# First cross attention of a two-layer block: two heads on 64 rows each, scores between two maxima, and one pair of maxima in eight copied by ScalarE

## The reference

```python
q = x @ Wq + bq            # x: 1024 rows of 128
k = y @ Wk + bk            # y: the context rows
v = y @ Wv + bv
scale = 1.0 / jnp.sqrt(D_HEAD)                 # D_HEAD = 16, 8 heads
weight = jnp.einsum('bhqd,bhkd->bhqk', q, k) * scale
weight = jax.nn.softmax(weight, axis=-1)
out = jnp.einsum('bhqk,bhkd->bhqd', weight, v)
return out.transpose(0, 2, 1, 3).reshape(B, SQ, D_EMBED) @ Wo + bo
```

## Time and profile before

| | us |
|---|---|
| median of 3 runs | 2700.87 |
| lowest and highest | 2694.35, 2701.8 |
| the profiled execution | 2705.45 |
| its span in the trace | 2703.7 |

### The profile page before, as it was taken

How to read it: one execution, slowest core, us unless ns; L and a number is a source line. 1 busy time by engine, 2 the same in 40 slices (tenths; PEclk the granted TensorE clock), 3 DMA queues, 4 the chain that set the end, 5 groups by cost and what they waited for, 6 DMA issues and landing times. The chain is left out here.

```text
span 2703.7 us, 33636 instructions
## 1 busy us (share of the span) xinstructions
PE 2405.5 (89%) x10214; PEld 876.6 (32%) x10272; DVE 2045.3 (76%) x3008; ACT 1513.5 (56%) x1842; POOL 301.9 (11%) x333
## 2 busy tenths in 40 slices
PE   6888677999999979999586599999999999997998
PEld 3555411222222224444222133323333333332443
DVE  5676688999995224344697888989999998976775
ACT  5555486777677843333332576666666666653111
POOL 5665500000000000000164000000000000000000
PEclk8898957999999989999698599999999999998998
DMA  5354371221000159954124331122013111111100
GB/s 144 127 167 143 130 113 31 67 63 31 26 24 27 31 104 211 217 153 121 32 73 98 78 91 30 30 63 72 29 30 105 30 30 30 30 36 69 47 1 8
DMA packets 200960, 198.63 MB, mean 73 GB/s; under 512 B 18525, under 2 KB 159362, under 8 KB 200086
## 3 DMA queue, kind: packets, MB, share of 16 engines
q1 hardware_dynamic: 200674, 196.69, 28.1%
q10 hardware_dynamic: 144, 0.10, 0.0%
HBM read 152.01 MB, written 41.48 MB: 72 GB/s over the span
## 5 line engine op out<-in xcount | busy, mean ns | idle before, releaser
L2768 DVE TENSOR_TENSOR y_acc<-y_acc,y_probs 128x1024 f32<-128x1024 f32 x400 | 486.7, 1217 | 35.2 <-ACT y_probs L2456 23.1
L2456 ACT ACTIVATE y_probs<-y_E,y_mask_bias 128x1024 f32<-128x1024 f32 x408 | 433.7, 1113 | 71.9 <-PE y_E L2548 63.9
L1223 ACT ACTIVATE x_probs<-x_E 128x1024 f32<-128x1024 f32 x408 | 397.1, 1024 | 135.8 <-PE x_E L1283 133.6
L1406 DVE TENSOR_REDUCE x_maxima<-x_M 128x1 f32<-128x496 f32 x660 | 410.2, 668 | 27.8 <-PE x_M L1265 17.2
L2557 PE MATMUL y_O<-y_probs,y_values 128*64 128x512 f32 x1632 | 400.2, 611 | 0.0
L2547 PE MATMUL y_E<-y_qa,y_ks 128*128 128x512 f16 x816 | 313.4, 384 | 1.5 <-ACT y_copied L2429 1.2
L2548 PE MATMUL y_E<-y_qb,y_ks 66*128 66x512 f16 x816 | 311.6, 382 | 0.0
L2429 ACT ACTIVATE y_copied<-y_M 128x1024 bf16<-128x1024 f32 (+1 forms) x164 | 162.5, 991 | 212.7 <-PE y_M L2511 212.7
L2706 DVE TENSOR_REDUCE y_maxima<-y_M 128x2 f32<-128x1024 f32 (+2 forms) x195 | 231.2, 1185 | 41.3 <-PE y_M L2511 32.3
L1874 DVE TENSOR_TENSOR f_hidden<-f_act_out,f_spread 128x512 f32<-128x512 f32 x160 | 110.7, 692 | 176.0 <-ACT f_act_out L1705 106.1
L1296 PE MATMUL x_O<-x_probs,x_values 128*32 128x512 f32 x1632 | 218.1, 607 | 0.7 <-ACT x_probs L1223 0.4
(11 more groups left out here) (499 smaller groups left out, 3154.6 us busy)
## 6 DMA issues: line engine op xcount, KB each, us to landing
f_spread<-comb_dram SPq DMA_DIRECT2D x160, 256.0 KB, 7.0
y_values<-v_dram SPq DMA_DIRECT2D x208, 128.0 KB, 2.2
v_dram<-a_v_out SPq DMA_DIRECT2D x26, 512.0 KB, 2.6
k_dram<-a_k_parts SPq DMA_DIRECT2D x26, 512.0 KB, 3.4
x_values<-v_dram SPq DMA_DIRECT2D x100, 128.0 KB, 2.2
f_weights<-f_w_in SPq DMA_DIRECT2D x40, 256.0 KB, 10.1
y_ks<-k_dram SPq DMA_DIRECT2D x75, 128.0 KB, 2.9
ssm_c_rows<-c_dram SPq DMA_DIRECT2D x16, 512.0 KB, 3.6
```

Source lines behind the costliest of these rows:

```text
L1223: nc.scalar.activation(probs[:, n % 2, 2 * g:2 * g + 2, :], psE[:, 2 * g:2 * g + 2, :], ACT.Exp).then_inc(exped, 1)
L1406: V.tensor_reduce(maxima[:, 2 * h + j, qt, c:c + 1], psM[(2 * entry + j) % 3][:, 0:CHUNK0], AX.X, ALU.max).then_inc(max_done, 1)
L2456: A(probs[:, i, :], psE[:, 2 * (i % 2):2 * (i % 2) + 2, :].rearrange("p a b -> p (a b)"), ACT.Exp, bias=mask_bias[:, bass.ds(c * TILES_IN_ ...
L2768: ins = V.tensor_tensor(acc[:, u % 2, :], acc[:, u % 2, :], probs[:, i, :], ALU.add)
```

## The change

There are four parts.

1. Keys and queries stand two heads together. A head has two groups of 64 rows, `low` 0 and 1, and the first head of a pair lies on partitions 0 to 63, the second on 64 to 127 (`row_place`). A score is then the sum of two matmuls on 64 rows (`low` 0 starts the bank, `low` 1 adds), and two heads run side by side: 8 matmuls on 64 rows in a tile take the place of 4 on 128. The maxima read `low` 0, and `qm` is gone. Loads of keys and queries are cut in two by head.
2. The order on TensorE in a tile is now: use, scores of the next tile (both g), use, values, and a third use if there is one.
3. A "max" use that is second in its tile, and whose pair is number 2 or 3 of 8, becomes "spare": ScalarE copies its two banks to bf16 (`copy_spare`, between its two exponentials of the next tile; two instructions where the banks don't adjoin), and VectorE merges the copy with one elementwise maximum into `spare_max`, in place of two reductions. There are 33 spares in the four units.
4. `give_maxima` gains a reduction of `spare_max` (units 1 to 3) and one or two memsets. GpSimd clears `spare_max`, three times.

```diff
                 def scores(u, t, g):
                     n = TILES0 * u + t
                     if n:
                         e.wait_ge(exped, 2 * n + g - 1)
-                    for j in (2 * g, 2 * g + 1):
-                        ins = T.matmul(psE[:, j, :], key_tile(4 * (u // 2) + j, t), qs[:, u, j, :],
-                                       start=True, stop=True)
-                    ins.then_inc(scored, 1)
+                    for low in range(2):
+                        for j in range(2):
+                            r = slice(64 * j, 64 * j + 64)
+                            ins = T.matmul(psE[:, 2 * g + j, :], key_tile(2 * (u // 2) + g, low, t)[r, :], qs[r, u, low, g, :],
+                                           start=(low == 0), stop=(low == 1))
+                            if low:
+                                ins.then_inc(scored, 1)
...
                 def free_banks(entry):
-                    e.wait_ge(max_done, max(2 * entry - 1, 0))
+                    for before in (entry - 2, entry - 1):
+                        if before in spare_number:
+                            e.wait_ge(spare_copied, spare_number[before] + 1)
+                    e.wait_ge(max_done, max(taken_before[entry] - ((entry - 1) not in spare_number), 0))
...
-                            scores(nu, nt, 0)
-                            if len(uses) == 3:
+                            if uses:
                                 use_banks(u, *uses.pop(0))
-                            scores(nu, nt, 1)
-                        if len(uses) == 2:
+                            for g in range(2):
+                                scores(nu, nt, g)
+                        if uses:
                             use_banks(u, *uses.pop(0))
                         weigh(u, t)
-                        if uses:
-                            use_banks(u, *uses.pop(0))
+                        for use in uses:
+                            use_banks(u, *use)
...
+                def copy_spare(entry):
+                    n = spare_number[entry]
+                    e.wait_ge(spare_mm, 2 * n + 2)
+                    if n >= 2:
+                        e.wait_ge(spare_merged, n - 1)
+                    out = spare[:, n % 2, :, :]
+                    banks = spare_banks(entry)
+                    heads = 2 // len(banks)
+                    for b, scores in enumerate(banks):
+                        ins = nc.scalar.activation(out[:, b:b + heads, :], scores[:, :, 0:CHUNK0], ACT.Copy)
+                    ins.then_inc(spare_copied, 1)
...
                         weights(u, t, 0)
+                        for kind, entry, _, _ in before[SPARE_AT:SPARE_AT + 1]:
+                            if kind == "spare":
+                                copy_spare(entry)
...
+                def merge_spare(n):
+                    e.wait_ge(spare_copied, n + 1)
+                    e.wait_ge(spare_cleared, spare_pair[n] // PAIRS)
...
+                    V.tensor_tensor(mine, mine, spare[:, n % 2, :, :], ALU.max).then_inc(spare_merged, 1)
...
+                def take_spares(u, entry):
+                    merge_spares_until(entry)
+                    e.wait_ge(spare_merged, spares_through(u))
+                    V.tensor_reduce(maxima[:, 0:4:2, 2:4, CHUNKS0].rearrange("p j q -> p q j"), spare_max[:], AX.X, ALU.max)\
+                        .then_inc(spare_taken, 1)
...
                         for kind, entry, pair_unit, pair in in_tile.get((u, t), ()):
+                            merge_spares_until(entry - 1)
```

More of the change, by code:

```diff
@@ L100, with row_place, load_queries, load_key_rows @@
 QS_ROWS = ((0, 0), (16, 1), (32, 0), (48, 0), (64, 2), (96, 1))
-QM_PARTS = (0, 1, 0)
-def load_far_queries(engine, k, d, u, loaded):
+LOW_ROWS = 64
+def row_place(r, head):
+    return r // LOW_ROWS, LOW_ROWS * head + r % LOW_ROWS
+def load_queries(engine, k, d, u, head, loaded):
     hg, cols = u // 2, slice(HALF * (u % 2), HALF * (u % 2) + HALF)
     rows = d.q0_dram[64 * hg:64 * hg + 64, :, cols]
[L108 to L119, removed]
-            .then_inc(loaded, 16)
[L123 to L138, removed]
+    for row, part in QS_ROWS:
+        low, r = row_place(row, head)
+        src = rows[:, part, :].rearrange("(h two f) n -> two f h n", f=16, two=2)[head]
+        engine.dma_start(k.qs[r:r + 16, u, low, :, :], src).then_inc(loaded, 16)
+def load_key_rows(sp, d, out, pairs, cols, row, part, loaded):
+    src = d.k0_dram[:, part, cols].rearrange("(h two f) n -> two f h n", f=16, two=2)
+    for head in range(2):
+        low, r = row_place(row, head)
+        sp.dma_start(out[r:r + 16, :, low, :], src[head][:, pairs, :]).then_inc(loaded, 16)
+def load_key_ones(sp, d, out, cols, loaded):
+    for head in range(2):
+        low, r = row_place(M_ROW0, head)
+        sp.dma_start(out[r:r + 16, :, low, :], d.key_ones[:, cols].unsqueeze(1).to_broadcast([16, 2, cols.stop - cols.start]))\
+            .then_inc(loaded, 16)
+KEY_PIECES = len(K_ROWS) + 1
 class Filler:
@@ L282, in _ @@
                 sp.dma_start(real[0:CTX, REST], d.real_keys[REST].partition_broadcast(CTX)).then_inc(spread_rest, 16)
[L283 to L286, removed]
+                for row in (80, 112):
+                    for head in range(2):
+                        low, r = row_place(row, head)
+                        sp.dma_start(k.qs[r:r + 16, :, low, :, :], d.x0_zeros).then_inc(zeroed, 16)
                 def store_k1(n):
@@ L1115, in _, with load_keys @@
             def _(sp):
-                def load_keys(heads, cols, loaded):
-                    for r, part in K_ROWS:
-                        load_key_rows(sp, d, ks[:, heads, cols], heads, cols, r, part, loaded)
-                    load_key_ones(sp, d, ks[:, heads, cols], cols, loaded)
-                near, far = slice(0, 4), slice(4, 8)
+                def load_keys(pairs, cols, loaded):
+                    for row, part in K_ROWS:
+                        load_key_rows(sp, d, ks[:, pairs, :, cols], pairs, cols, row, part, loaded)
+                    load_key_ones(sp, d, ks[:, pairs, :, cols], cols, loaded)
+                near, far = slice(0, 2), slice(2, 4)
                 sp.wait_ge(k.q_rest, 32)
```

137 lines of the change are left out of this document (88 added, 49 removed).

## The result

The changed kernel takes **2725.66 us** (median of 4 runs, 2723.55 to 2729.05), against 2699.43 us for the kernel before in as many runs: a ratio of 1.0096, interval 1.0076 to 1.0117. It is 26.2 us slower, where the forecast was 16.0. The profiled execution took 2726.0 us, its span 2724.0.

A forecast was written before the change was run, and what follows sets the result against it. TensorE was taken to set the tile, VectorE 0.24 us behind. Terms -19.0 - 0.6 + 29.0 + 6.6 = +16.0 us took the median from 2700.87 to 2716.9 us, 8-in-10 range 2690 to 2738.

The forecast's parts named there:

- the end of the maxima: End of each unit's maxima: TensorE waits for the 2.2 us reduction and memsets; +6.6 us in sum, bounds 2 to 8.
- the plain tile: Two-maxima tile in units 0 to 2: 2.43 us instead of 2.60, -19.0 us over 112 tiles.
- unit 3: Unit 3 keeps its loop between scores and exponentials, alternating 2.20 and 1.97 us; no change, stays at 109 us.
- 64 rows and order, units 0 to 2: Two shape-change gaps vanish on TensorE: -19.0 us in 112 plain tiles, -0.6 us in twelve three-maxima tiles.
- The spare: ScalarE's copy between exponentials and VectorE's merge delay TensorE: 0.59 + 0.27, say 0.88 us each, +29.0 us for 33.
- The three waits: Behind a spare: next maxima at 2.83 instead of 2.43 us, second scores 3.73 instead of 3.47, merge 0.27 more.
- A: At spares: next maxima and second scores don't wait for the copy; sum -13.0 us, 2688 us; chance 0.17.
- B: At spares: only the wait for the copy costs, 33 x 0.40 = 13.2 us; sum +0.2, 2701 us; chance 0.25.
- C: On TensorE: gaps stay between equal 64-row shapes, so rows and order gain nothing; 2736 us; chance 0.10.
- D: On TensorE: weight loads on 64 rows show, making a tile 0.45 us longer; 2785 us; chance 0.03.
- The signs: Expected in the trace: VectorE's share in units 0 and 1 from 94% to about 88%, each lasting about 150 us.
- The loads: Twice as many key pieces of half size, hidden by 12 us ahead of first use: cost nothing; uncovered, 1 or 2 us.

The follow-up runs named there:

- the ends alone: Changed kernel with no pair copied or merged, but the 1,984-element reduction and GpSimd's clears kept: 2705.82 us, ratio 0.9994 to the kernel before.
- the shorter end: Changed kernel with the merge one entry earlier, GpSimd's memset behind the split, and the spare_max reduction in three steps: 2716.17 us, ratio 1.0053 to before.

## Why the forecast was right in kind and 10 us short

The sign, the mechanism and the range held (2725.7 in 2690 to 2738). Of the four terms of the sum the end of the maxima was badly off and the plain tile slightly; unit 3, forecast unchanged, was off too. This is the sum with what the stretches and tiles gave, the gain from before to the kernel without spares, the losses from that to the changed one:

| term | forecast | measured |
|---|---|---|
| 64 rows and order, units 0 to 2 | -19.6 | -15.3 |
| the same, unit 3 | 0 | +1.1 |
| spares | +29.0 | +26.0 |
| end of the maxima | +6.6 | +12.5 |
| first tile, and rounding | 0 | +0.7 |
| sum | +16.0 | +25.0 |

**The plain tile, 2.43 forecast, 2.46 found.** Its reasoning held: maxima to scores is 0.22 (662.83 to 663.05), so equal shapes have no gap, and the second maxima wait for the hand-over of the bank, 1.15 us behind the first (1.14 forecast). The last term was misread. Values to the next maxima is 629.00 to 630.00 in the earlier trace rows, 1.00 us, and is 1.00 here (664.29 to 665.29); I took 0.98 "less rounding", which no row gives. With the 0.01 of the hand-over that is 0.03 us, over 112 tiles 3.4 us, most of the term's miss. Another 0.6 is the tiles with three maxima, which kept their 3.62 us where 3.57 was forecast. The measured -15.3 and +26.0 are themselves uncertain by about 1 us each, as the profiled execution without spares was spared the low clock at the start of unit 0. Of two readings of the same row, the shorter was the one I hoped for.

**Unit 3, forecast unchanged, 1.1 us longer.** Its longer step is 2.23 us in the mean of 21 tiles (890.91 to 893.15, below, is one of 2.24) instead of 2.21, which is half of the 1.1; the rest is some 0.1 us in each of the few tiles that are longer anyway. The shorter step stays 1.97. Unit 3 is the same without spares, so the difference comes with the 64-row scores. Why the loop between scores and exponentials is 0.02 us longer stays open.

```profile
885.92 1.07 PE L1343 MATMUL x_O<-x_probs,x_values 128*32 128x512 f32 x8
...
887.89 1.07 PE L1343 MATMUL x_O<-x_probs,x_values 128*32 128x512 f32 x8
...
890.91 1.06 PE L1343 MATMUL x_O<-x_probs,x_values 128*32 128x512 f32 x8
...
893.15 1.06 PE L1343 MATMUL x_O<-x_probs,x_values 128*32 128x512 f32 x8
```

**The spare, 0.88 forecast.** Measured 0.84 with a one-instruction copy (3.05 and 2.71 against twice 2.46) and 0.90 with two. The three waits are where they were placed: next maxima 2.91 us behind the first (2.83), the tile after the next at 5.81 (5.72), and the merge at 0.26 in its own experiment (0.27). The total is smaller than 33 times that, because four spares are not paid for so: two in the last tile of a unit cost nothing, as no maxima wait behind them, and two lie in the tile behind an end and are counted there. The other 29 took 26.0 us, 0.90 each. So the term came out 3.0 us too high, which hid a part of what the ends cost more; that is luck. Where the tile behind has 3.13 us, the merge costs 0.39, not 0.25.

**The end, 6.6 forecast, 12.5 found: the step that failed.** The 2.22 us of reduction was right. I took it, with 0.2 for the memsets, for the whole price of the ends of unit 1's and unit 2's maxima, which lie in units 0 and 1. In place of 2.4 us they took 5.4 and 5.6, each over two tiles, and the sum went past the upper bound of 8. Of the first tile's 4.63, counted from start to start, 2.26 is the reduction, 0.17 VectorE's own memset, and 1.03 the cast that GpSimd's memset held up. I had said that GpSimd's memsets "stand behind nothing that waits", and looked only for who waits for GpSimd, not for what shares its ports. The remaining 1.17 us is TensorE's clock. Windows from the first maxima behind the wait to the values, the same 13 matmuls, of the changed kernel and then of the one without spares:

```profile
568.85:571.50 2.65, 2.65 (x13) 0.75 (x13) 1.78 (x3) 1.02 (x1) 0.00 (x0) 0.50 0.00 0
```

```profile
554.02:555.50 1.48, 1.48 (x13) 0.50 (x13) 1.48 (x3) 0.59 (x1) 0.00 (x0) 1.00 0.00 0
```

At a granted clock of 0.50, which is 1.2 GHz, the piece takes 2.65 us, at 1.00 it takes 1.48. TensorE had idled 4.99 us ahead of the one and 1.53 ahead of the other, which the timeline without spares shows:

```profile
554.02 0.38 PE L1298 MATMUL x_M<-x_keys,qs 64*128 64x496 bf16 x2 [1.53 <-DVE x_maxima L1450]
```

The low clock held from 566.3 to 573.2, so it began while TensorE still idled:

```profile
566.35:573.15 6.80, 4.30 (x20) 0.95 (x20) 4.08 (x10) 2.54 (x3) 0.63 (x1) 0.50 0.00 0
```

The kernel before has a short one at the start of unit 0 (447.1 to 450.5), and the changed one has it too, but the kernel before has none at the ends.

```profile
447.15:450.50 3.35, 3.35 (x12) 0.74 (x16) 2.18 (x4) 1.86 (x2) 0.00 (x0) 0.50 0.17 49
```

There the change made a wait long enough that the clock fell, and so was paid for twice. With the wait at 3.96 us, and at 3.57, it fell too, for 3.4 us in unit 0. Third end: 1.46 instead of 1.4.

**The rivals.** A (spares free, 2688) and B (only the copy's wait, 2701) fell with the halved spares and the moved merge: three waits, each with its price. ScalarE's idle share spoke for A and meant nothing, as the forecast said. The measured time lies halfway between the forecast and C (the gaps stay, 2736), yet nothing of C is in it: its mark, 0.31 us from maxima to scores, is not there, and the kernel without spares is faster than before, where C has no gain. A time that nearly fits proves nothing. D (weight loads in the open, 2785) fell as well: eight loads lie within 0.74 us beside scores that take no longer than four of 128 rows (663.05, 1.03 us for eight; 1.04 in the earlier trace rows). The rule of the Trainium skill, "TensorE: Matmul & The Clock Gate", section "Part 3: Packing small matmuls — row/col tiling", that a weight load overlaps matmuls only in another row group, is not borne out: each score pair loads over the row groups that the pair ahead of it uses, and nothing of it shows.

The signs: VectorE's share was to fall to 88% and fell to 83%, units 0 and 1 were to last 150 us and lasted 153. The error in the lengths is the ends' and the tile's. It doesn't explain the share: VectorE's 127.3 us of work would be 85% of 150 us too, and the forecast shows no sum for its 88%.

**The loads, forecast at nothing.** Nothing of them is seen: the first values of unit 0 start at 435.66 us of the execution, before the change at 435.79.

## What to carry to other kernels

An engine that is idle 30% of the time is no place to put work if the work holds a buffer: ask when the buffer comes free, in the order in which that engine gets to it, and multiply by the count. Where a change holds several edits, price and run each alone; here the 64 rows gave 0.5%, the order nothing, and the spares with their end took 1.5% away. When something is added to a point at which all engines wait, count what else the longer wait sets off: a TensorE idle for 3.6 to 5 us came back at half clock, and a clear on GpSimd that nobody waited for held up VectorE.

## What the runs showed of the hardware

- **GpSimd against VectorE.** A GpSimd memset of 1,984 bf16 elements (1.75 us) held a VectorE cast from f32 to bf16 in SBUF, 0.17 us by itself, up to 1.20 us, and one to 1.38 in the kernel with the ends alone (556.65, below). VectorE's reduction of f32 in SBUF that began 0.02 us ahead of it (565.21, 0.39 us), VectorE's own memset of 52 elements beside it (565.67, 0.10 us), and four reductions from PSUM were not held up. The cast of the kernel with the ends alone:

```profile
556.65 1.38 DVE L1524 CAST x_mpart<-x_mneg 128x16 bf16<-128x16 f32 x1
```

- **The clock.** At the ends in units 0 and 1, where TensorE was busy for 87 to 94% of the unit, every idle of 3.57 to 5.08 us came with 3.4 or 6.8 us at a granted clock of 0.50, and every one of 1.44 to 1.61 us with none. The length of the idle doesn't say which of the two: 4.99 us came with 6.8 in the changed kernel, 4.98 with 3.4 where the merge was moved; 3.57 came with 3.4 in unit 0 and 3.66 with 6.8 in unit 1 of one and the same execution, that of the shorter end. Near the start of unit 0, soon after the clock had come up from 0.50, an idle of 1.90 to 2.04 us was followed by 3.4 us at 0.50 in some executions (the kernel before, the changed one) and not in others (no spares, the ends alone), so a short idle is not safe everywhere.
- **Shapes on the array.** Going from 64-row maxima to 64-row scores costs nothing (0.22 us for 496 columns), where 64 to 128 rows cost 0.10 us. A plain tile lost two of its four shape changes and went from 2.60 to 2.46 us, 0.14 less. The first gave 0.10 us; the second can't be seen by itself, since the maxima behind the scores now wait for their bank.
